# A wavelength-multiplexed attention kernel on one core: VectorE takes all 2048 columns of channel 14's last key tile in units 0 to 15

## What is computed

```python
def wl_step(acc, wl):
    cpm, iw = wl
    m = cpm[None, :, None, None]
    Qw = Q * m
    Kw = K * m
    scores = jnp.einsum('bhqd,bhkd->bhqk', Qw, Kw) * SCALE
    scores = scores * jnp.cos(KERR * scores * scores)
    attn = jax.nn.softmax(scores, axis=-1)
    out = jnp.einsum('bhqk,bhkd->bhqd', attn, V)
    return (acc + out * iw, None)
acc, _ = jax.lax.scan(wl_step, acc0, (cos_pm, interference_weights))
```

## Time and profile before

| | |
|---|---|
| median of 3 runs | 3453.41 us (3448.43 to 3458.12) |
| the profiled execution, its time | 3451.96 us |
| its span, first to last instruction | 3449.9 us |
| ScalarE busy | 3334.6 us, 97% |
| VectorE busy | 3152.2 us, 91% |
| TensorE matmuls busy | 2711.8 us, 79% |
| mean granted TensorE clock | 0.909 |
| line 656, whole exponentials | 3101.2 us busy, 447 of them |
| line 653, the shorter one | 202.5 us busy, 32 of them |

### The profile page before, as it was taken

One profiled execution on the slowest core, in us unless ns is written; L12 is line 12 of the kernel. 1 busy time (PEld: TensorE's weight loads), 2 busy tenths in 40 slices (PEclk: granted clock), 3 DMA queues, 4 the chain that ended last, 5 costly groups with the idle time before them and its releaser, 6 DMA issues.

```text
span 3449.9 us, 47792 instructions
## 1 busy us (share of the span) xinstructions
PE 2711.8 (79%) x20599; PEld 778.2 (23%) x20599; DVE 3152.2 (91%) x2977; ACT 3334.6 (97%) x610; POOL 199.5 (6%) x325
## 2 busy tenths in 40 slices
PE   7887778887778887778887788887888887888763
PEld 2222222222222222222222222222222222222222
DVE  8899899899899899899899999999999999999977
ACT  7999999999999999999999999999999999999971
POOL 0000000000000000000010011110011110011111
PEclk8899999999999999999999999999999899999886
DMA  1000000000000000000000000000000000000010
GB/s 50 1 1 1 1 1 1 1 1 1 1 1 1 1 1 1 1 14 1 1 3 1 4 2 4 2 4 1 2 4 2 4 2 1 4 2 4 2 30 28
DMA packets 20759, 16.10 MB, mean 5 GB/s; under 512 B 4225, under 2 KB 18962, under 8 KB 20306
## 3 DMA queue, kind: packets, MB, share of 16 engines
q1 hardware_dynamic: 19282, 12.34, 1.2%
q10 hardware_dynamic: 1152, 0.53, 0.1%
q0 software_dynamic: 128, 0.26, 0.0%
HBM read 7.76 MB, written 5.37 MB: 4 GB/s over the span
## 4 chain that ended last, share of the span: by engine, by line
ACT 61%; issue 30%; ACTq 4%; DVE 3%; PE 2%; DMA 0%; SPq 0%; POOL 0%; DVEq 0%; POOLq 0%
ACT probs L656 56%; ACT probs L653 4%; ACTq L646 4%; PE psum L1273 1%; DVE m_pad L865 0%; ACTq L650 0%; DVE s_t L877 0%; ACT probs L680 0%; DVE probs L1190 0%; DVE probs L928 0%; DMA iw<-nterference_weights_dram 0%; SPq L468 0%; DVE x_p L743 0%; DVE x_p L735 0%; DVE x_p L739 0%
## 5 line engine op out<-in xcount | busy, mean ns | idle before, releaser
L656 ACT ACTIVATE probs<-s_t 128x8192 f32<-128x8192 f32 x447 | 3101.2, 7090 | 2.2 <-PE psum L1273 2.2
L1273 PE MATMUL psum<-probs,v_pad 128*27 128x512 f32 x15232 | 1992.5, 665 | 602.5 <-ACT probs L656 583.8
L1273 PEld LDWEIGHTS psum<-probs,v_pad 128*27 128x27 f32 x15232 | 485.3, 115 | 2036.1 <-issue 1095.5
L723 DVE SCALAR_TENSOR_TENSOR x_y<-s_t,c_last,x_2k 128x2048 f32<-128x2048 f32 (+1 forms) x160 | 344.1, 2150 | 2.3
L735 DVE SCALAR_TENSOR_TENSOR x_p<-x_p,x_y 128x2048 f32<-128x2048 f32 (+1 forms) x160 | 332.6, 2079 | 4.5
L743 DVE SCALAR_TENSOR_TENSOR x_p<-x_p,x_2k 128x2048 f32<-128x2048 f32 (+1 forms) x160 | 332.1, 2075 | 3.9
L731 DVE SCALAR_TENSOR_TENSOR x_p<-x_y 128x2048 f32<-128x2048 f32 (+1 forms) x160 | 330.9, 2068 | 3.3 <-PE psum L756 3.3
L739 DVE SCALAR_TENSOR_TENSOR x_p<-x_p 128x2048 f32<-128x2048 f32 (+1 forms) x160 | 331.5, 2072 | 2.4
L877 DVE COPY s_t<-psum 128x2048 f32<-128x2048 f32 x128 | 292.2, 2284 | 21.8 <-PE psum L839 21.1
L865 DVE TENSOR_REDUCE m_pad<-psum 128x4 f32<-128x2048 f32 x128 | 292.4, 2286 | 10.8 <-PE psum L802 9.7
L756 PE MATMUL psum<-x_p,v_pad 128*27 128x512 f32 x1152 | 174.5, 620 | 51.9 <-DVE x_p L743 51.4
(11 more groups left out here) (240 smaller groups left out, 1116.0 us busy)
## 6 DMA issues: line engine op xcount, KB each, us to landing
s_t<-in_L_attn_x_dram SPq DMA_DIRECT2D x4, 256.0 KB, 6.9
x_next_dram<-x_p SPq DMA_DIRECT2D x1, 1024.0 KB, 4.5
x_group<-x_next_dram SPq DMA_DIRECT2D x1, 1024.0 KB, 4.9
loop_memory<-in_L_attn_x_dram SPq DMA_DIRECT2D x8, 128.0 KB, 2.2
x_dram<-loop_memory SPq DMA_DIRECT2D x8, 128.0 KB, 1.8
out_dram<-loop_memory SPq DMA_DIRECT2D x8, 128.0 KB, 1.8
x_dram<-probs SPq DMA_DIRECT2D x2, 512.0 KB, 3.3
out_dram<-probs SPq DMA_DIRECT2D x2, 512.0 KB, 3.6
```

Of the source, the lines that this page charges most:

```text
L656: nc.scalar.activation(probs[:, (p + w) % 2, :], s_t[:, p, :], ACT.Exp, scale=scales[(p + w) % 2]).then_inc(s["exp_done"], 1)
L723: nc.vector.scalar_tensor_tensor(out=y, in0=scores, scalar=scale, in1=at, op0=ALU.mult, op1=ALU.subtract) \
L1273: last = nc.tensor.matmul(products_of(u, wg)[L * b:L * b + SLOTS * A, :], v_pad[:, p, b * T + kt, c0:c0 + SLOTS * A], probs[:, (p + w) % 2 ...
```

## The change

`SHARED_B` becomes a pair, one value for each group: 0 in units 0 to 15, 2 as before in units 16 to 31, and `ACT_LAST` a list with it: 6144 columns and 7168. In units 0 to 15 ScalarE's exponential of channel 14 thus covers three key tiles and none of the fourth, and piece 4 of VectorE covers the fourth key tile whole, with 2048 columns in each of its seven operations. TensorE takes all four batches of that key tile from `x_p`, and none of them from `probs`. The order of slots stays as it was.

```diff
--- before.py
+++ after.py
@@ -40,8 +40,8 @@
 W_GROUPS = [(0, 3), (3, 3), (6, 3), (9, 3), (12, 3), (15, 1)]
 WA = W - 1
 X_COLS = NB * S
-SHARED_B = 2
-ACT_LAST = T * X_COLS - (NB - SHARED_B) * S
+SHARED_B = (0, 2)
+ACT_LAST = [T * X_COLS - (NB - b) * S for b in SHARED_B]
 PIECES = T + 1
 
 
@@ -650,7 +650,7 @@
                         act.wait_ge(s["pv_done"], u * WA + (w + 2))
                         if w == WA - 1:
 
-                            nc.scalar.activation(probs[:, (p + w) % 2, 0:ACT_LAST], s_t[:, p, 0:ACT_LAST], ACT.Exp,
+                            nc.scalar.activation(probs[:, (p + w) % 2, 0:ACT_LAST[g]], s_t[:, p, 0:ACT_LAST[g]], ACT.Exp,
                                                  bias=ln_one[:, 0:1], scale=scales[(p + w) % 2]).then_inc(s["exp_done"], 1)
                             continue
                         nc.scalar.activation(probs[:, (p + w) % 2, :], s_t[:, p, :], ACT.Exp,
@@ -711,7 +711,7 @@
 
             piece, base = u * PIECES + n, (u * PIECES + n) * PIECE_LINKS
 
-            w, start, cols = (W - 1, n * X_COLS, X_COLS) if n < T else (WA - 1, ACT_LAST, T * X_COLS - ACT_LAST)
+            w, start, cols = (W - 1, n * X_COLS, X_COLS) if n < T else (WA - 1, ACT_LAST[u // H], T * X_COLS - ACT_LAST[u // H])
             scores = s_t[:, p, start:start + cols]
             scale = c2_last[:, w - (WA - 1), h:h + 1]
             at, y, t = x_n[:, 0:cols], x_y[:, 0:cols], x_p[:, 0:cols]
@@ -751,8 +751,8 @@
                 pe.wait_ge(s["o_copied"], max(u * NWG + 1, 2))
             wg, kt = (NWG - 1, n) if n < T else (LAST_OF[WA - 1], T - 1)
             c0 = VPAD if n < T else VPAD - A * SLOT_OF[WA - 1]
-            for b in range(NB) if n < T else range(SHARED_B, NB):
-                at = b * S if n < T else (b - SHARED_B) * S
+            for b in range(NB) if n < T else range(SHARED_B[u // H], NB):
+                at = b * S if n < T else (b - SHARED_B[u // H]) * S
                 last = nc.tensor.matmul(products_of(u, wg)[L * b:L * b + SLOTS * A, :],
                                         v_pad[:, u % 2, b * T + kt, c0:c0 + SLOTS * A],
                                         x_p[:, at:at + S], start=(n == 0), stop=(n == T - 1 or (n == T and u < UNITS - 1)))
@@ -1268,13 +1268,13 @@
                             pe.wait_ge(s["o_copied"], max(u * NWG + (wg + 1 if wg >= 2 else 2 * wg), 2))
                         c0 = VPAD - A * SLOT_OF[w]
                         for kt in range(T):
-                            for b in range(SHARED_B if w == WA - 1 and kt == T - 1 else NB):
+                            for b in range(SHARED_B[g] if w == WA - 1 and kt == T - 1 else NB):
                                 at = (kt * NB + b) * S
                                 last = nc.tensor.matmul(
                                     products_of(u, wg)[L * b:L * b + SLOTS * A, :], v_pad[:, p, b * T + kt, c0:c0 + SLOTS * A],
                                     probs[:, (p + w) % 2, at:at + S],
                                     start=(kt == 0 and w in FIRST_OF),
-                                    stop=(w in LAST_OF and kt == (T - 2 if u == UNITS - 1 and w == WA - 1 and b >= SHARED_B else T - 1)))
+                                    stop=(w in LAST_OF and kt == (T - 2 if u == UNITS - 1 and w == WA - 1 and b >= SHARED_B[g] else T - 1)))
                         last.then_inc(s["pv_done"], 1)
                         for v, at in due(u, w, TURN_STEPS, LAST_TURN_STEPS):
                             turn_products(v, at)
```

## The result

The changed kernel takes 3479.43 us (median of 4 runs, 3476.49 to 3482.31) against 3450.92 us for the kernel before, run beside it (4 runs, 3447.97 to 3458.12): a ratio of 1.0079, 95% interval 1.0059 to 1.0100, some 28 us slower. Its profiled execution took 3476.61 us with a span of 3474.5 us, where the one before had 3451.96 and 3449.9.

The account below looks back on a forecast made before the run. ScalarE alone was taken to bound the kernel at 103.08 us a unit; VectorE's 101.6 + 2.7 = 104.3 us would replace it, so 3.3 us once plus 15 units at 1.25 made +22 us: 3475 us, range 3454 to 3489.

Parts of the forecast that it names:

- ScalarE then waits ahead of its tenth exponential: Sign in units 1 to 15: gaps of about 2 us on ScalarE, released by TensorE, there or at the fourth.
- ScalarE's 0.77 us for 1024 columns: Channel 14's exponential, units 0 to 15: 0.77 us saved each, 12.3 us in all; upper end 0.87 us.
- VectorE's 6.1 us more: Fifth piece, units 0 to 15: seven operations on 2048 columns add 6.1 us, making VectorE's own work 101.6 us.
- The waits that can't go, 2.7 us: VectorE at slots 9 and 10: waits of 1.23 and 1.50 us stay, making its unit 104.3 us.
- Unit 26 of the kernel before: Nearest row to a late VectorE: slot 7's matmuls 4.88 us, VectorE waiting 2.73 us at slots 9 and 10.
- a round trip between VectorE and TensorE at slot 10: VectorE ends piece 2, TensorE does product, matmuls, transposes; the reciprocal's wait, 3.48 us in unit 6, moves along.
- The clock: TensorE's granted clock falls behind waits for VectorE; slot 7's matmuls cost 1.7 us more, counted once in unit 1.
- Rival B: Clock stays up at slot 9, VectorE waits only 1.50 us: unit 103.1 us, total 3457 us; chance 0.19.
- 3.3 us once in unit 1: Unit 0's late fifth piece delays unit 1: 4.4 us plus 1.7 for slot 7's clock, less 2.8 of margin.
- Unit 16: Units 16 to 31 stay as they were; VectorE's late entry into them costs nothing, up to 3 us.
- Rival D: VectorE's extra work fits into its waits at slots 10 and 7, ScalarE stays the bound: 3441 us; chance 0.08.
- Rival C: Longest waits hold, slot 10 keeps its 3.48 us: unit 105.1 us, +33 us, 3487 us; chance 0.18.

Follow-up runs that it names:

- experiment 11: The changed kernel with two matmuls whose result nobody reads added in slot 6 alone, units 1 to 15: 3457.4 us, ratio 1.0019.
- experiment 7: The changed kernel with the third polynomial step of piece 2 cut to 2 columns in units 0 to 15: 3475.3 us, ratio 1.0068.
- experiment 5: The changed kernel with unused matmuls added, three in slot 0 and two in slot 6, units 1 to 15: 3455.1 us, ratio 1.0013.
- experiment 1: The kernel before with only VectorE's fifth piece widened to the whole last key tile in units 0 to 15: 3478.8 us, ratio 1.0081.
- Experiment 3: The change by half against the kernel before: VectorE takes 1536 columns, ScalarE 6656, in units 0 to 15: 3443.0 us, ratio 0.9980.
- experiment 10: The kernel before with unused matmuls added in slots 0 and 6 of units 1 to 15: 3450.0 us, ratio 0.9997.

## Why the prediction was right, and where its steps were not

It said 3475 us, slower, in a range of 3454 to 3489; measured were 3479.4. The loss itself was forecast at 22 us; it was 28.5 by the medians, since the kernel before came out at 3450.9 beside it, and 24.6 between the two profiled spans. The mechanism was right in this: ScalarE's relief is small, VectorE's added work and the waits that it can't give up set the pace, and ScalarE then waits ahead of its tenth exponential. Where the waits come from was right in part only. Term by term:

- *ScalarE's 0.77 us for 1024 columns* was too small: 0.84 measured, near the upper end of 0.87. The form with a bias carries a little more fixed cost, as the text allowed. The Trainium skill (ScalarE: Activation LUTs, Rules for kernel authors) gives 0.83 ns an element; the estimate of 0.85 us from it was the better price.
- *VectorE's 6.1 us more* gave 101.6 us of its own; 101.4 was measured. The steps of the polynomial took 2.28 to 2.30 us.
- *The waits that can't go, 2.7 us*, were 3.2. Unit 26 of the kernel before was the right row to price them by: its slot 7 at 4.88 us came back as 5.31, and its waits of 1.23 and 1.50 us at slots 9 and 10 as 1.13 and 1.50 in the unit behind the one shown above. A unit took 104.66 us against 104.3 forecast. VectorE's timeline there:

```profile
736.65 2.29 DVE L877 COPY s_t<-psum 128x2048 f32<-128x2048 f32 x1 [1.13 <-PE psum L839]
...
741.63 0.46 DVE L1422 RECIPROCAL r_z<-psum 128x48 f32<-128x48 f32 x1 [1.50 <-PE psum L1243]
```

- *What those waits are* was told rightly for one state of the clock only. The text called them a round trip between VectorE and TensorE at slot 10, "However late VectorE comes, this wait goes with it". With slot 7 at full clock it is so: in units 3 and 12 of the changed kernel, and in all 15 of experiment 11, the chain comes back over piece 2's product and slot 10's matmuls. In the other 13 units the path has left VectorE at piece 1. In unit 5, slot 10's product waited 0.59 us for VectorE, but its matmuls then waited for the eleventh exponential, which the tenth had delayed; experiment 7 agrees, as 2.2 us less on VectorE ahead of slot 10 left the unit's time as it was. There the wait is the time that the path spends elsewhere. That the sum came out is in part luck: unit 26, from which the 2.7 us were read, contained the whole path, whatever I called it.
- *The clock* stood in the sum only as 1.7 us once and inside the 2.7. It was in truth the term that decides a unit's balance: with the clock up the unit takes 102.9 us, under the 103.08 of the kernel before (the whole stayed 0.1 to 0.2% slower, as unit 16, without added matmuls, took 104.4 us in experiment 11 and 107.1 in experiment 5). Rival B had just this number (unit 103.1, 3457) and experiments 5 and 11 reached it (3455 and 3457), but only with matmuls added for the purpose. Left alone, the clock did as unit 26 showed. The rows don't tie it to the length of the gap alone. Behind a wait of 2.91 us slot 7 ran in part at 1.2 GHz in unit 2 and at 2.4 GHz throughout in unit 3. Behind one of 1.93 us slot 9 was at the lower clock in part in unit 26, while behind the same 1.93 us it took 3.64 us in unit 5 (626.40). The Trainium skill (TensorE: Matmul & The Clock Gate, Why this matters for your kernels) asks that idle gaps between bursts stay short; these rows are of short gaps with either outcome, so the rule doesn't decide this case.
- *3.3 us once in unit 1* was 0.5 us (103.61 us, 131.32 to 234.93). The clock did fall in its slot 7, but I had left ScalarE's relief in unit 0 (0.84 us) out of the margin, and VectorE came out of unit 0's slot 10 earlier, with a shorter wait than the 3.48 us that unit 0 of the kernel before shows there too: its reciprocal starts at 114.97 behind a wait of 2.43 us, and at 117.70 in the kernel before. Up to there the two kernels do the same work, so these 2.7 us are a difference between two executions: chance, and not the change. In experiments 1 and 7 unit 1 took 105.8 and 105.6 us, some 2.6 us over the kernel before, so the 3.3 us wasn't far off where that chance was missing.

  Unit 16 cost 2.6 us, which I had priced at nothing, up to 3. From ScalarE's exponential of channel 14 at its start to that at its end are 1805.40 - 1699.73 = 105.67 us: it still inherits unit 15's late piece 4. The sum of what was measured: 0.5 + 14 x 1.55 (104.63 in the mean of units 2 to 15) + 2.6 = 24.8 us, against 24.6 us between the two spans.
- *Rival D* (fits into the waits) had the right threshold, 102.3 against 101.6, and the wrong side of it. Experiment 3 is that rival, at half the columns: VectorE's 98.3 us and the same kind of waits leave ScalarE alone. *Rival C*'s 105.1 is what two of three units show (105.1 to 105.4), with one of 103.5 to 103.8 behind them.

What stays open is what decides the clock in a given unit, and with it why the units come in threes, two long and one short. Between units 2 and 3 the whole difference is that of slot 7's matmuls at one clock and at the other. In units 6, 9 and 15 slot 7 was at the lower clock too, but slot 1 was not, and piece 1 came 1.3 to 1.4 us earlier. With the added matmuls slot 7 is at full clock in every unit and no unit of 3 to 14 takes over 103.3 us.

## What to carry to other kernels

An engine at 91% busy can have nothing left to give: read its waits one by one, and ask of each whether the other side waits for this engine in turn, directly or over a third engine. When work is moved off the bound, try half of it first; here 512 columns a unit gained 8 us and 1024 lost 28. Cut the same amount of work in two places of the order: if only one of them moves the time, the loop that sets the pace runs through that one.

## What the hardware showed that I had not expected

Work without use made the kernel faster. Two matmuls of 128x512 (1.88 us together) in a gap of 3 us ahead of slot 7 kept the granted clock at 1.00, where it had been 0.68, and made the 32 matmuls behind it take 3.62 us, not 5.31; 15 units of this won some 21 us of 3479. Where ScalarE didn't wait for the work whose clock they raised (slot 10 in the kernel before, experiment 10), the time stayed the same. A second set ahead of work that the first had already brought to full clock in most units (slot 0, experiment 5 against 11) added nothing that can be told.
